# Two graph-convolution passes: the rows of the first four edge blocks of each source tile come from one-hot products on TensorE instead of gathers on GpSimd

## The reference

```python
# _L2_gnn_ref, with dst, src = edge_index[0], edge_index[1]
feat_n = feature[src] * relation_weight
seg_sum = jax.ops.segment_sum(feat_n, dst, num_segments=n)
neigh_mean = seg_sum / jnp.maximum(seg_cnt, 1.0)
return jnp.concatenate([feature, neigh_mean], axis=-1) @ W + b
# _L3_gnn_ref, with row, col = edge_index[0], edge_index[1]
msgs = norm[:, None] * x[col]
agg = jax.ops.segment_sum(msgs, row, num_segments=n)
return agg @ W.T + b
# the end of the network
h = jnp.maximum(_layernorm(x, axis=-1), 0.0)
x = x + _L2_gnn_ref(h, edge_weight1, L2_gnn_W, L2_gnn_b, edge_index)
h = jnp.maximum(_layernorm(x, axis=-1), 0.0)
x = x + _L3_gnn_ref(h, edge_index, L3_gnn_W, L3_gnn_b)
```

## Time and profile before

| | |
|---|---|
| runs | 11020.37 us median of 3 (11018.97 to 11024.36) |
| profiled execution, span | 8504.6 us, 106528 instructions |
| PE busy | 3426.3 us (40%) |
| DVE busy | 3575.8 us (42%) |
| ACT busy | 2245.1 us (26%) |
| POOL busy | 5889.8 us (69%) |

### The profile page before, as it was taken

How to read it: one execution, slowest core, us unless ns; L and a number is a source line. 1 busy time by engine, 2 the same in 40 slices (tenths; PEclk the granted TensorE clock), 3 DMA queues, 4 the chain that set the end, 5 groups by cost and what they waited for, 6 DMA issues and landing times. The chain is left out here.

```text
span 8504.6 us, 106528 instructions
## 1 busy us (share of the span) xinstructions
PE 3426.3 (40%) x18282; PEld 3028.2 (36%) x18283; DVE 3575.8 (42%) x13136; ACT 2245.1 (26%) x6884; POOL 5889.8 (69%) x6182
## 2 busy tenths in 40 slices
PE   5434443444434344434333354454542333323333
PEld 4234443444434344434322342333322333323233
DVE  7455553455533555433333355777751111111111
ACT  0212222322223222223222233555532222200000
POOL 0467777577776777766777746777747777677777
PEclk9566666666667666667666677777766666666666
DMA  0322222122221222211222213333322222122222
GB/s 21 93 48 53 54 54 55 42 53 54 53 54 43 51 54 53 54 49 49 54 54 54 55 40 110 105 105 105 105 70 54 55 58 55 53 55 58 55 55 55
DMA packets 374250, 509.70 MB, mean 60 GB/s; under 512 B 217568, under 2 KB 259556, under 8 KB 373796
## 3 DMA queue, kind: packets, MB, share of 16 engines
q0 software_dynamic: 212288, 464.41, 20.5%
q1 hardware_dynamic: 149854, 38.28, 2.1%
q10 hardware_dynamic: 11978, 5.55, 0.3%
HBM read 458.78 MB, written 49.00 MB: 60 GB/s over the span
## 5 line engine op out<-in xcount | busy, mean ns | idle before, releaser
L1625 POOL DMA_INDIRECT rows<-table_d,meta x3200 | 3035.5, 949 | 1013.2 <-issue 894.2
L1685 PE MATMUL ps_total<-weighted_rows,ident 128*128 128x129 f32 (+1 forms) x8000 | 1733.8, 397 | 2495.8 <-ACT weighted_rows L1708 2006.7
L1685 PEld LDWEIGHTS ps_total<-weighted_rows,ident 128*128 128x128 f32 x8000 | 1558.3, 275 | 2665.2 <-issue 2556.5
L1827 DVE SCALAR_TENSOR_TENSOR prod<-rows,q_rows 128x129 f32<-128x129 f32 x3200 | 928.5, 294 | 2120.4 <-DMA rows<-table_d,meta 1584.0
L1470 PE MATMUL tile_sums<-tile_rows,sums 128*128 128x129 f32 x3332 | 609.7, 366 | 1504.8 <-ACT tile_rows L1407 766.4
L1470 PEld LDWEIGHTS tile_sums<-tile_rows,sums 128*128 128x128 f32 x3332 | 592.4, 279 | 1524.5 <-issue 1510.6
L1269 POOL DMA_INDIRECT tile_rows<-table_d,tile_halves x833 | 789.9, 948 | 266.3 <-issue 253.6
L1269 POOL DMA_INDIRECT tile_rows<-rows_d,tile_halves x833 | 789.3, 948 | 265.4 <-issue 253.7
L1708 ACT ACTIVATE weighted_rows<-rows,power 128x129 f32<-128x129 f32 x3200 | 959.4, 389 | 6.5
L1625 POOL DMA_INDIRECT rows<-pairs_d,meta x800 | 774.9, 969 | 257.9 <-issue 243.2
L1702 ACT ACTIVATE power<-expo 128x17 f32<-128x17 f32 x200 | 43.6, 218 | 3020.9 <-DVEq L1860 3020.9
(11 more groups left out here) (569 smaller groups left out, 4756.8 us busy)
## 6 DMA issues: line engine op xcount, KB each, us to landing
rows<-table_d,meta POOLq DMA_INDIRECT x3200, 2.5
tile_rows<-table_d,tile_halves POOLq DMA_INDIRECT x833, 2.5
tile_rows<-rows_d,tile_halves POOLq DMA_INDIRECT x833, 2.5
rows<-pairs_d,meta POOLq DMA_INDIRECT x800, 2.8
meta<-list_in_d SPq DMA_DIRECT2D x250, 32.0 KB
words<-words_in_d SPq DMA_DIRECT2D x250, 0.0 KB
resets<-resets_in_d SPq DMA_DIRECT2D x250, 8.0 KB
table_d<-em_h ACTq DMA_DIRECT2D x7, 448.0 KB, 4.7
```

Source lines behind the costliest of these rows:

```text
L1625: pool.indirect_dma_start(rows[q][:, j, 0:width], None, table_d, bass.IndirectOffsetOnAxis(meta[q][:, j, number:number + 1], 0)).then_inc( ...
L1685: mm = pe.matmul(total[:, q, ds(part, 1), 0:W].rearrange("p a w -> p (a w)"), k.ident[:], wide[:, j % WS, :], start=False, stop=True, skip ...
L1827: own(dve.scalar_tensor_tensor(prod[:, j, :], rows[q][:, j, :], -1.0, asked, ALU.mult, ALU.mult, accum_out=score[:, j, :]))
```

## The change

The list by source tile is now made from the edges in their given order (three loads in the histogram stage into `so.src`, `so.dst` and `so.facts`, in place of the copies from the first layout), so that within a tile's region the edges stand in the order of `dst`. The first four blocks of a tile then read rows from a short span of the table. `WINDOWS` names for each of these blocks a first tile and a number of tiles (5, 6, 7 and 8, 26 in all; other firsts for the last tile).

A new stage, `near_edges`, runs once after `place_rest`. It reads the first 512 list entries of each tile, and for each works out the row's place inside its window (`near_window_d`), the lane and the weight (`near_facts_d`). An edge outside its window stays in a second list, and if there is any, `sweeps` is 2 and each pass runs a second time over that list. With these inputs no edge of the first 512 of a tile lies outside its window (worked out from `src` and `dst`).

In `tile_pass`:

- GpSimd gathers 13 blocks of a tile (`FARC`) instead of 17.
- SP loads for each tile the 512 places (2 KB), repeated on all 128 partitions (256 KB on the SBUF side). In "weigh" it also loads the whole of `k.x` again (49 tiles).
- VectorE compares them with the window's row numbers (`window_of`, in PSUM): 26 one-hot matrices for each tile in four instructions (`spread_windows`), a tile ahead, in batches of 13 matrices over three buffers. The one-hot matrices for the sums are made in two instructions, 4 and 13.
- TensorE multiplies these 26 with the table in SBUF (`k.q`, and in "sum" `k.x`), which gives the rows of four blocks in PSUM (`gather`). It then sums 4 + 13 products.
- ScalarE copies the 4 blocks from PSUM to SBUF (`near_rows`), with the weight in "weigh".
- "weigh" writes its result to `k.x` and `made_d`, and "sum" writes its own to `k.q`, in place of two small buffers and `k.x`.

```diff
+WINDOWS = ((0, 5), (2, 6), (4, 7), (7, 8))
+WINDOWS_LAST = ((0, 5), (3, 6), (6, 7), (9, 8))
+NEAR = len(WINDOWS)
+NEARP = NEAR * P
+FARC = GC - NEAR
+BATCHES = ((0, 3), (1, 2))
+BATCH = 13
+HOTS = 3
...
# tile_pass, SP
+                    def rows_of_window(t):
+                        if t >= 2:
+                            sp.wait_ge(m["near_hot"], len(BATCHES) * (t - 1))
+                        sp.dma_start(window[t % 2].rearrange("p c j -> p (c j)"),
+                                     so.window_d[ds(e * T + t, 1)].rearrange("a n -> (a n)").partition_broadcast(P)
+                                     ).then_inc(windowed[t % 2], 16)
...
+                    if weigh:
+                        sp.dma_start(k.x[:], residual_d.rearrange("(t p) c -> p t c", p=P)).then_inc(m["residual"], 16)
...
# GpSimd
-                        for c in range(GC):
+                        for c in range(FARC):
                             pool.indirect_dma_start(rows[b][:, c, 0:P], None, table_d, bass.IndirectOffsetOnAxis(meta[:, t, c:c + 1], 0)
...
# VectorE
+                    def spread_windows(t):
+                        dve.wait_ge(windowed[t % 2], 16 * (t // 2 + 1))
+                        for i, columns in enumerate(BATCHES):
+                            n = len(BATCHES) * t + i
+                            if n >= HOTS:
+                                dve.wait_ge(m["gathered"], n - HOTS + 1)
+                            at = 0
+                            for c in columns:
+                                w = WINDOWS[c][1]
+                                ins = dve.tensor_tensor(near_hot[n % HOTS][:, at:at + w, :], window[t % 2][:, c].unsqueeze(1).to_broadcast([P, w, P]),
+                                                        window_of[:, 0:w].unsqueeze(2).to_broadcast([P, w, P]), ALU.is_equal)
+                                at += w
+                            ins.then_inc(m["near_hot"], 1)
...
# ScalarE, ahead of the weights of tile t
+                        if t < T:
+                            act.wait_ge(m["gathered"], len(BATCHES) * (t + 1))
+                            if t >= 2:
+                                act.wait_ge(m["summed"], t - 1)
...
+                            if weigh:
+                                for c in range(NEAR):
+                                    ins = act.activation(near_rows[q][:, c, 0:P], taken[:, c, :], ACT.Copy, scale=near[:, 1, t, c:c + 1])
+                            else:
+                                ins = act.copy(near_rows[q][:, :, 0:P], taken)
+                            ins.then_inc(m["near_rows"], 1)
...
# TensorE
+                    def gather(t):
+                        if t:
+                            pe.wait_ge(m["near_rows"], t)
+                        for i, columns in enumerate(BATCHES):
+                            n = len(BATCHES) * t + i
+                            pe.wait_ge(m["near_hot"], n + 1)
...
+                                for j in range(w):
+                                    mm = pe.matmul(gathered[:, c * P:(c + 1) * P], near_hot[n % HOTS][:, at + j, :],
+                                                   table[:, first + j, 0:P], start=(j == 0), stop=(j == w - 1), skip_group_check=True)
...
+                    gather(0)
                     for t in range(T + 2):
...
+                        if t + 1 < T:
+                            gather(t + 1)
```

More of the change, by code:

```diff
@@ L227, in one_hots, with histogram @@
                              ALU.is_equal)
-def histogram(nc, k, oh, deg):
+def histogram(nc, k, oh, deg, so, src, dst, weight):
     with ExitStack() as s:
-        m = open_stage(nc, s, ["hot", "hot_used", "zeroed", "summed"])
+        m = open_stage(nc, s, ["hot", "hot_used", "zeroed", "summed", "natural"])
         zero = buf(nc, s, "hist_zero", [P, P], BF16)
@@ L948 @@
 GC = 17
-PARTS = (0, 6, 11, 15, 17)
+PARTS = (0, 5, 9, 12, 13)
 CHUNK = P * GC
@@ L1011, in _ @@
                 own = Steps(dve, m["own"])
-                own(dve.memset(so.hi, -1.0))
-                own(dve.memset(so.facts, 0.0))
                 own(dve.memset(so.keep[:], 1.0))
@@ L1183, in tile_pass @@
                                "unpacked", "prepared", "turned_ps", "turned", "multiplied", "new_taken", "stat", "rooted", "scaled",
-                               "made", "stored0", "stored1"] + [f"listed{g}" for g in range(NGT)] + [f"got{b}" for b in range(RB)]
+                               "made", "stored0", "stored1", "near_listed", "window0", "window1", "near_hot", "gathered", "near_rows",
+                               "residual"]
+                       + [f"listed{g}" for g in range(NGT)] + [f"got{b}" for b in range(RB)]
                        + ["late_weighted"]
@@ L1206, in tile_pass @@
         if weigh:
-            made = [buf(nc, s, f"tile_made{q}", [P, TG, P]) for q in range(2)]
             stats = buf(nc, s, "tile_stats", [P, TG, 6])
@@ L1216, in tile_pass @@
         total = psum(nc, s, "tile_sums", [P, 2, 512], F32)
-        order = psum(nc, s, "tile_order", [P, P], F32)
+        fixed = psum(nc, s, "tile_fixed", [P, 512], F32)
+        order, window_of = fixed[:, 0:P], fixed[:, P:P + 8]
+        gathered = psum(nc, s, "near_gathered", [P, 512], F32)
         turned_ps = psum(nc, s, "tile_turned", [P, TG, P], F32)
@@ L1237, in _ @@
                     dve.memset(rows[b][:, :, P:P + 1], 1.0)
-        with nc.Fori(0, turns) as e:
+                for q in range(2):
+                    dve.memset(near_rows[q][:, :, P:P + 1], 1.0)
+        with nc.Fori(0, turns) as e, nc.Fori(0, again) as again_i:
             with nc.Block() as block:
@@ L1318, in finish @@
                         if not weigh:
-                            own(dve.tensor_tensor(k.x[:, ts, :], new[:, 0:n, :], k.h[:, ts, :], ALU.add))
+                            own(dve.tensor_tensor(k.q[:, ts, 0:P], new[:, 0:n, :], k.h[:, ts, :], ALU.add))
                             own.wait()
@@ L1460, in _ @@
                                 pe.wait_ge(m["taken"], t - 1)
+                            pe.wait_ge(m["near_rows"], t + 1)
+                            for c in range(NEAR):
+                                pe.matmul(total[:, q, 0:P + 1], spare[:, q, c, :], near_rows[q][:, c, :], start=(c == 0), stop=False)
                             if t < T - 1 and weigh:
@@ L2929, in gnn_kernel @@
         k.dis = buf(nc, c, "root_degree", [P, T])
-        tile_pass(nc, k, "weigh", k.table_d, so.regions_d, chunks, k.rows_d)
-        tile_pass(nc, k, "sum", k.rows_d, so.regions_d, chunks, out_d)
+        tile_pass(nc, k, "weigh", k.table_d, so, chunks, sweeps, k.made_d, k.rows_d)
+        tile_pass(nc, k, "sum", k.made_d, so, chunks, sweeps, out_d)
 def fill_runs(dve, own, k, t, records):
```

253 lines of the change are left out of this document (211 added, 42 removed).

## The result

The changed kernel takes 10762.0 us (10751.39 to 10782.12, 4 runs), the kernel before 11022.37 beside it: ratio 0.9768, 95% interval 0.9754 to 0.9782, 260 us faster. The forecast was 10564, with a range up to 10700: the direction was right, the size was not.

A forecast was written before the change was run, and what follows sets the result against it. GpSimd's gathers were taken to bound both passes, before and after. Gathers -491.1, `near_edges` +33, passes' starts +4 and setup -2 gave -456 us, so 11020.4 became 10564; range 10420 to 10700.

The forecast's parts named there:

- If it is fixed (a launch, say), the time is 11020.4 - 456 = 10564: Whole program: time beyond the profiled span stays unchanged, so the span's 456 us gain comes off the measured time.
- The 2515.8 us: Whole program: the median of the runs above the profile's span, which no row explained; the forecast took it as fixed.
- So GpSimd stays the bound: Both passes: GpSimd's 13 gathers, 16.3 us a tile, set the pace, with 3 to 4 us a tile beneath it.
- the sum: Span: gathers -491.1, new stage +33, passes' starts +4, setup -2, together -456 us, from 8504.6 to about 8049.
- the passes' starts: Start of both passes: more constants, fills, a register and an inner loop, +2 us each, +4 (0 to 8).
- Rival 4: Whole program: the time beyond the span goes with the work, so the span's ratio holds for all: 10430 us; 17%.
- Rival 1: Both passes: TensorE at half clock sets the pace, 19.1 us a tile instead of 16.3, +274, 10838 us; 7%.
- Rival 3: Both passes: the windows hold GpSimd up 4.1 us in each of 98 tiles, +402, 10966 us; 3%.
- `near_edges`: New stage between two barriers, hidden behind nothing: +33 us, between 20 and 50.
- The gathers' pace beside the windows: Both passes: GpSimd's gathers beside a busier VectorE cost 0, with +20 us kept for the range.
- The lower end of the forecast's own range: Whole program: 10535 us, with no cost beyond 20 for the new stage and nothing else.
- TensorE's 12 to 13 us a tile: Both passes: 43 products, some 10 at half clock and 33 at full, plus group ends; under GpSimd's 16.3 us.

The follow-up runs named there:

- c1_before: The kernel before, unchanged, run again on the second chip (late): 10989.76 us, ratio 0.9997.
- d1: The changed kernel, unchanged, on the third chip (late): 10734.89 us, ratio 0.9766 to the kernel before.
- f1: The changed kernel without gathers in "sum" (far rows a constant), on the fourth chip (late): ratio 0.9294 to the kernel before.
- b1_before: The kernel before, unchanged, run again on the first chip (on time): 8497.51 us, ratio 0.9997.
- d2: The kernel before without blocks 0 to 3 of each tile in gathers, weights and sums, third chip (late): 10433.17 us, ratio 0.9487.
- c3: The changed kernel with the windows' comparison reading both inputs from SBUF, second chip (late): 10731.95 us, ratio 0.9765 to the kernel before.
- b3: The changed kernel, unchanged, on the first chip (on time): 8035.10 us, ratio 0.9454 to the kernel before.
- d4: The changed kernel with each group of window products done twice, third chip (late): 11354.64 us, ratio 1.0326 to the kernel before.

## Why the prediction was wrong, point by point

- **The step that failed** is "If it is fixed (a launch, say), the time is 11020.4 - 456 = 10564". The 2515.8 us are no part outside the program: the timed executions have longer spans. From c1_before and the earlier trace rows they lie in all stages with gathers: "weigh" begins 2,180 us later, and the two passes take 1,176 and 1,170 us where they took 1,043 and 1,042. What makes them in a pass is that TensorE starts instructions 0.7 and 1.4 us late while gathers stream: 4,515 records, 255 late starts with gathers and none without (d1, f1). Most of the 2,480 us between b1_before and c1_before lie ahead of the passes, 1,589 from the first to the last gather of the attention layers and 510 in the relation layer. No experiment touched these, and VectorE is late there too, so for them the cause is carried over from the passes and not shown.
- **"So GpSimd stays the bound"** holds on time alone. In the late executions a tile of the kernel before takes 24.0 us (c1) and not 21.3, since TensorE held GpSimd up, and one of the changed kernel takes 20.2 to 21.1 and not 16.3. Between c1 and d1 the time from the first gather to the end falls from 2426.7 to 2102.6 us, -324 where the sum had -487 (gathers and the passes' starts). This term, mis-sized by 163 us, makes most of the 196 us between the forecast gain (456) and the measured one (260); some 30 more are the relation layer's (below).
- **Rival 4** ("not fixed but go with the work", 10430) named the right doubt with the wrong mechanism. It scaled everything; the lateness belongs to TensorE's instructions under gathers, and the change adds 26 of its products a tile. d2 shows what the rival would have given had it been gathers alone: 10433. The near work took 302 us of that back.
- **Rival 1** (TensorE sets the pace) came true in the late executions, but not at half clock: 0.75 over the passes, against 0.84 on time and 0.98 where TensorE never idles (f1).
- **Rival 3** (the windows hold GpSimd up) did not come true: with one input in PSUM a gather beside the windows takes 0.95 us, as elsewhere (d1). Its mechanism is real with both inputs in SBUF, but smaller than it was priced: 96 us of gathers' time in two passes (c3) and not 402.
- **The sum itself**: the kernels on time give -464 us where it has -456. `near_edges`, from the last record of `place_rest` to the relation layer's weights, took 28.7 us more than the gap before (37.8 less 9.1) where I took 33, and 27.6 in the late d1. The gathers' pace beside the windows (0 taken, up to 20 feared) was 0. The lower end of the forecast's own range was added up wrongly: no cost beyond 20 for the stage gives 11020.4 - 491.1 + 20 - 2 = 10547, and not 10535.
- **TensorE's 12 to 13 us a tile**: 12.4 to 12.5 on time, which was right; 10.2 where it never idles (f1).
- **Left open**: the gathers of the relation layer, which the sum had at no change, take longer with the changed kernel on late chips: 1553.9 us from the first to the last against 1526.2 on the second chip (c3, c1), 1560.6 against 1536.9 on the third (d1, d2); on time it is 1014.3 against 1016.0 (b3, b1). No run explains these 24 to 28 us. Why some chips are late, and whether a steady stream of plain transfers would do the same there, was not settled; the one run meant for it met an on-time chip.

## What to carry to other kernels

Compare the profile's span with the median of the runs before any sum: where they are 2.5 ms apart, the trace is of another kind of execution than the times, and every "engine X has room" read in it must be asked again. A change that moves work from a gathering GpSimd to TensorE pays in full only where TensorE's instructions start on time (464 us); on late chips it paid 260 us, and TensorE gets its pace back only in GpSimd's pauses, 3.5 to 9 us into them. An unchanged time does not show that an edit costs nothing: look at the instructions themselves, as in c3, where slack hid 96 us.

## What the runs showed of the hardware

- On three of four chips, and in the first timed runs, TensorE starts instructions 0.7 or 1.4 us late in a stream of indirect transfers from GpSimd, from 8.5 us or more after it begins to 3.5 us after its last gather (medians of d1 and d4; 9.0 in the kernel before); VectorE's share of idle time "issue" grows too (`prod`, 486.9 us on time, 3191.1 late), a register operation takes TensorE's queue 179 ns in the mean against 36 on time and VectorE's 156 against 44, but ScalarE's 35 in both. It goes with the gathers: 255 late starts in a pass with 13 a tile, 43 with 7, none with 0. Whether their number, their density or the missing pause counts was not told apart.
- A gather takes 944 to 949 ns in both kinds, with the same packets; only its effect on the other engines differs.
- Beside a VectorE comparison with both inputs in SBUF a gather takes 1.26 us in the mean (304 in c3); beside one with an input in PSUM it takes 0.95 (380 in d1).
